# The key bias of the last attention's scores: from one-row products on TensorE to a fused add and maximum on VectorE

## What is computed

```python
qp = jnp.einsum('bsf,gf->bsg', q, Wq) + bq
kp = jnp.einsum('bsf,gf->bsg', k, Wk) + bk
vp = jnp.einsum('bsf,gf->bsg', v, Wv) + bv
attn = jax.nn.softmax(jnp.einsum('bqf,bkf->bqk', qp, kp), axis=-1)
return jnp.einsum('bqk,bkf->bqf', attn, vp) + q
```

## Time and profile before

| | |
|---|---|
| median of three runs | 1693.21 us (1687.25 to 1696.94) |
| the profiled execution | 1693.78 us |
| its span, first to last instruction | 1692.0 us |
| granted TensorE clock, mean | 0.977 |
| TensorE (PE) busy | 1595.8 us, 94% |
| VectorE (DVE) busy | 1112.9 us, 66% |
| ScalarE (ACT) busy | 991.6 us, 59% |
| GpSimd (POOL) busy | 271.6 us, 16% |

### The profile page before, as it was taken

One profiled execution on the slowest core, in us unless ns is written; L12 is line 12 of the kernel. 1 busy time (PEld: TensorE's weight loads), 2 busy tenths in 40 slices (PEclk: granted clock), 3 DMA queues, 4 the chain that ended last, 5 costly groups with the idle time before them and its releaser, 6 DMA issues.

```text
span 1692.0 us, 33823 instructions
## 1 busy us (share of the span) xinstructions
PE 1595.8 (94%) x12897; PEld 1029.4 (61%) x12897; DVE 1112.9 (66%) x2221; ACT 991.6 (59%) x2024; POOL 271.6 (16%) x344
## 2 busy tenths in 40 slices
PE   6789999999999999999999999999999989998987
PEld 5444445575767657575766657565656656564766
DVE  4566786867677676867677686867667675834433
ACT  3345667666667566656666666565756555664342
POOL 5200312021212011121203011100011010101110
PEclk9989999999999999999999999999999999997979
DMA  6913242536131331536131331336131320303200
GB/s 184 217 56 122 72 79 70 111 84 123 48 86 32 88 69 55 113 82 125 44 97 30 83 71 55 83 81 118 39 74 33 66 62 29 78 29 74 52 32 13
DMA packets 171647, 129.37 MB, mean 76 GB/s; under 512 B 40751, under 2 KB 161885, under 8 KB 171229
## 3 DMA queue, kind: packets, MB, share of 16 engines
q1 hardware_dynamic: 171421, 127.19, 32.0%
q10 hardware_dynamic: 64, 0.02, 0.0%
HBM read 78.92 MB, written 47.71 MB: 75 GB/s over the span
## 4 chain that ended last, share of the span: by engine, by line
PE 76%; DVE 11%; DMA 4%; ACT 4%; issue 2%; SPq 2%; DVEq 0%; ACTq 0%; POOLq 0%; POOL 0%
PE ps_o L1663 12%; PE ps_max L1634 11%; PE ps_s L1651 10%; PE ps_last L1582 10%; PE ps_last L1591 6%; DVE mxh L1320 6%; PE ps_pre L1446 4%; PE ps_cross L1550 4%; PE ps_pre L1454 3%; PE ps_cross L1536 3%; DMA den<-o_s 2%; PE ps_last L1454 2%; DVE mx L1248 2%; PE ps_last L1620 1%; PE ps_last L1604 1%
## 5 line engine op out<-in xcount | busy, mean ns | idle before, releaser
L1320 DVE TENSOR_REDUCE mxh<-ps_max 128x1 f32<-128x512 f32 x1024 | 655.6, 682 | 200.7 <-PE ps_max L1634 198.6
L1104 ACT ACTIVATE probs<-ps_s 128x512 f32<-128x512 f32 x1024 | 577.3, 596 | 235.4 <-PE ps_s L1651 177.5
L1634 PE MATMUL ps_max<-kst,qst 96*128 96x512 bf16 x1024 | 375.5, 388 | 23.3 <-DVE mxh L1320 16.9
L1651 PE MATMUL ps_s<-qst,kst 98*128 98x256 bf16 x2048 | 374.7, 276 | 11.0 <-ACT probs L1104 8.9
L1651 PEld LDWEIGHTS ps_s<-qst,kst 98*128 98x128 bf16 x2048 | 176.2, 98 | 162.4 <-ACT probs L1104 49.1
L1663 PE MATMUL ps_o<-probs,vg 128*17 128x256 f32 x4096 | 266.0, 382 | 0.0
L1634 PEld LDWEIGHTS ps_max<-kst,qst 96*128 96x128 bf16 x1024 | 97.1, 97 | 138.1 <-DVE mxh L1320 95.0
L1048 ACT ACTIVATE probs<-ps_cross 77x512 f32<-77x512 f32 x224 | 133.1, 594 | 72.5 <-PE ps_cross L1536 71.3
L1280 DVE SCALAR_TENSOR_TENSOR th<-th,gb 128x256 f32<-128x256 f32 x128 | 61.4, 480 | 160.4 <-ACT gb L1079 160.4
L1663 PEld LDWEIGHTS ps_o<-probs,vg 128*17 128x17 f32 x4096 | 97.7, 97 | 106.9 <-issue 43.6
L1582 PE MATMUL ps_last<-y_hi,wff_hi 128*128 128x256 f32 x448 | 139.9, 312 | 5.2 <-DVE y_lo L1274 4.3
(11 more groups left out here) (265 smaller groups left out, 2021.4 us busy)
## 6 DMA issues: line engine op xcount, KB each, us to landing
parts_s<-qk_parts SPq DMA_DIRECT2D x28, 384.0 KB, 3.9
o_s<-o_sb SPq DMA_DIRECT2D x64, 128.0 KB, 2.8
o_s<-o_sb SPq DMA_DIRECT2D x32, 256.0 KB, 2.2
oT<-o_s SPq DMA_DIRECT2D x62, 128.0 KB
den<-o_s SPq DMA_DIRECT2D x62, 128.0 KB
kst<-parts_s SPq DMA_DIRECT2D x16, 384.0 KB, 5.3
kst<-parts_s SPq DMA_DIRECT2D x48, 128.0 KB, 6.0
qst<-parts_s SPq DMA_DIRECT2D x64, 96.0 KB, 2.6
```

The source lines that it names most:

```text
L1104: nc.scalar.activation(probs[:, step % PR, 2 * pair:2 * pair + 2, :].rearrange("p j q -> p (j q)"), ps_s[pair][:, :], ACT.Exp, scale=SCALE ...
L1320: nc.vector.tensor_reduce(mxh[:, i // 2, i % 2:i % 2 + 1], ps_max[i % 2][:, :], AX_X, ALU.max).then_inc(g_mx, 1)
L1634: mm(ps_max[i % 2][:, :], qst[0:ROWS, h, q * P:(q + 1) * P], kst[0:ROWS, h, half * 512:(half + 1) * 512], start=True, stop=True).then_inc( ...
L1651: last = mm(ps_s[pair][:, j * CH:(j + 1) * CH], kst[:, h, kt * P:(kt + 1) * P], qst[:, h, :], start=True, stop=True)
```

## The change

The bias row is loaded to all 128 partitions, by a broadcast, instead of to one. The two one-row products of a chunk are gone, and so is the row of ones. On VectorE the reduction over both halves of the bank is replaced by two fused calls, one for each tile: each adds `m3_b` to the scores in PSUM, writes the sum back to the same place, and gives the maximum along the row into a column of `mx3`. As VectorE now reads `m3_b`, its next load waits for the last maximum of the preceding chunk (`c_mx3`) on SP.

```diff
-        ones = sb("ones", [1, P])
...
-        m3_b = sb("m3_b", [1, CTX])
+        m3_b = sb("m3_b", [P, CTX])
...
-                sp.dma_start(m3_b[:, :], m_s[D:D + 1, :].rearrange("a (b n) -> b a n", b=B)[b]).then_inc(c_tab, 16)
+                sp.wait_ge(c_mx3, o * TT)
+                sp.dma_start(m3_b[:, :], m_s[D:D + 1, :].rearrange("a (b n) -> b (a n)", b=B)[b].partition_broadcast(P)
+                             ).then_inc(c_tab, 16)
...
-            nc.gpsimd.memset(ones[:, :], 1.0).then_inc(s_const, 1)
...
-                nc.vector.tensor_reduce(mx3[:, :], bank_[:, :].rearrange("p (i n) -> p i n", i=TT)[:, :, 0:CTX],
-                                        AX_X, ALU.max).then_inc(c_mx3, 1)
-                dve.wait_ge(c_mx3, o + 1)
+                for i in range(TT):
+                    scores3 = bank_[:, i * CH:i * CH + CTX]
+                    nc.vector.tensor_tensor_reduce(scores3, scores3, m3_b[:, :], 1.0, -3.0e38, ALU.add, ALU.max,
+                                                   accum_out=mx3[:, i:i + 1]).then_inc(c_mx3, 1)
+                dve.wait_ge(c_mx3, (o + 1) * TT)
...
-                        mm(bank_[:, i * CH:i * CH + CTX], den2s[e][:, k, i * P:(i + 1) * P], m3[:, k, :],
-                           start=(k == 0), stop=False)
-                    last = mm(bank_[:, i * CH:i * CH + CTX], ones[:, :], m3_b[:, :], start=False, stop=True)
+                        last = mm(bank_[:, i * CH:i * CH + CTX], den2s[e][:, k, i * P:(i + 1) * P], m3[:, k, :],
+                                  start=(k == 0), stop=(k == KD - 1))
```

More of the change, by code:

```diff
@@ L790, in _ @@
             nc.gpsimd.memset(neghalf[:, :], -0.5).then_inc(s_const, 1)
-            nc.gpsimd.memset(ones[:, :], 1.0).then_inc(s_const, 1)
             v = v_sb[:, :, :, :]
             nc.gpsimd.memset(v, 0.0).then_inc(s_const, 1)
-            pool.wait_ge(s_const, 5)
+            pool.wait_ge(s_const, 4)
             nc.gpsimd.memset(v[:, :, :, DH:DH + 1], 1.0).then_inc(s_const, 1)
@@ L921, in _ @@
             act.wait_ge(s_cols, 1)
-            act.wait_ge(s_const, 6)
+            act.wait_ge(s_const, 5)
             def head():
```

## The result

Four executions of the changed kernel took 1666.29 to 1672.34 us, median 1667.69; four of the kernel before, on the same chip, had a median of 1693.46. The ratio is 0.9857 (95% interval 0.9821 to 0.9892), which is 24.2 us less. Two later comparisons gave 0.987 and 0.9864, 22.0 and 23.0 us less. The direction was right and the size too small.

The account below looks back on a forecast made before the run. TensorE was taken to bound the kernel (76% of the chain). Block gains of 15.4 us less 0.9 for the load gave 14.5, from 1693.78 to 1679.3 us; range 1671 to 1689.

Parts of the forecast that it names:

- TensorE's saving: Score blocks without one-row groups: 2.35 us falls to 1.17 in steady stages, 1.18 less; 1.19 less under LATE.
- The sum: Whole kernel: 8 x 1.16 + 4 x 0.95 + 3 x 0.78 = 15.4 us, less 0.9 for the bias load, gives 14.5.
- VectorE's pair: Two fused calls with maximum reads replace one 0.48 us reduction: 2 x (0.34 + 0.10) = 0.88 us, 0.40 more.
- The covers: VectorE's slack before TensorE needs the banks of the following maxima: 0.38 us in steady stages, 0.16 under LATE.
- `FINAL`'s 0.78: Chunk under FINAL: the values group waits for ScalarE's exponential, so 0.40 us is lost and 0.78 kept.
- The load: Bias row to 128 partitions on SP's queue delays the inverse sums' broadcast: 0.9 us charged once; bounds none and 3.6.
- The clock: Whole kernel: the forecast sum had no term for granted clock; more or fewer dips stood only among the rivals.
- Rival 1: VectorE's calls cost the upper price, so banks of the next maxima come late in 12 stages: 1687.9 us, chance 0.14.
- Rival 2: Next stage's projection waits for normalised rows set by SP's queue; six stages give nothing: 8.8 us gain, 1685.0, chance 0.12.
- Rival 3: Faster TensorE waits into half clock in eight more steady and LATE stages, 3.8 us each: 1709.7 us, chance 0.05.
- Rival 4: Two fewer dips of the clock than before: 1671.7 us, chance 0.08.
- the low price: VectorE's two calls at 2 x 0.34 us, reads hidden, 0.20 more than now; with a free load 1677.0 us.

Follow-up runs that it names:

- TensorE's part alone: Kernel before without the one-row products, nothing in their place, bias missing, old single reduction and one-partition load kept: 1671.09 us, ratio 0.9886 to before.
- VectorE's part alone: Changed kernel with each tile's one-row product put back, weights of zero; fused calls and broadcast load stay: 1691.46 us, ratio 1.0004 to the kernel before.
- the load later: Changed kernel with the bias row's broadcast moved behind the broadcast of the inverse sums on SP's queue: 1673.34 us, ratio 0.9891 to the kernel before.

## Why the prediction was right or wrong

**TensorE's saving: right.** Forecast 1.18 us a chunk, measured 1.20 and 1.21. The way it was found also held: the price of a group is read to the start of what follows it, and the time between records of one kind gives what remains when the other kind goes.

**The sum: the step that failed.** Sixteen blocks at 1.18 us are 18.9 us of TensorE time, and the sum let 14.5 of them reach the end: it took off 3.5 us as new waits for VectorE, ScalarE and the GELU chain at the blocks, and 0.9 for the load. New waits there are, some 2.2 us in all (below), but TensorE's idle time over the whole span did not grow: 96.2 us before, and in the three profiled executions of the change 96.1, 1663.6 - 1571.8 = 91.8 and 1668.9 - 1572.6 = 96.3. What TensorE waits more at the blocks it waits less elsewhere, so the whole of the 18.9 reached the end; where elsewhere is not settled, as such waits differ by some us from one execution to the next. The runs agree: TensorE's part alone, without VectorE's calls and the load, was no faster than the change. The second step that failed is that the clock was taken to stay as it was: it gave 2.8 us (0.8 to 4.8). Together with the mean of the idle time, 1.5 us less, these make 18.9 + 1.5 + 2.8 = 23.2, beside the 22.0 to 24.2 of the three comparisons.

**VectorE's pair: its price was mis-sized.** The step put 0.40 us on it. The calls take 0.18 more than the reduction did (0.69 against 0.51), just under the low bound of 0.20, and they start 0.09 later behind TensorE's next group, for which the step had no term: 0.27 together. The single call's 0.34 us was right:

```profile
L1295 DVE DVE_READ_ACCUMULATOR2_ANT mx<- x32: 137/140/142, 392.0 to 1662.4; 128x1 f32 x32
L1295 DVE CUSTOM_DVE_ANT_0 ps_last<-ps_last,m_b x30: 326/341/358, 391.8 to 1662.1; 128x154 f32<-128x154 f32 x30
```

These are ns of one, least, median and most. The read takes 0.14 us, but the next call starts with it, 0.25 us after the first call and so ahead of the first call's own end; only the last read stands alone. The Trainium skill, "VectorE: DVE Perf Modes", "Two Vector instructions with no wait between them", says that an operation that also writes out its accumulator is two instructions; the trace shows both. The prediction's estimate from that page, 0.95 us for the pair, adds their lengths; the trace has 0.69 from the first call to the next operation, since they overlap.

**The covers: right.** Those of 0.38 and 0.16 us stand. With 0.27 in place of 0.40, `LATE` pays 0.27 - 0.16 = 0.11, and 0.12 was measured; `ENDING` keeps 1.19 - 0.27 = 0.92, as measured. `FINAL`'s 0.78 came out to the digit, and chunk 14 gave 0.1, forecast nothing. The terms at the blocks become 8 x 1.20 + 4 x 1.09 + 0.78 + 0.92 + 0.1 + 0.96 = 16.7 us instead of 15.4, which leaves 18.9 - 16.7 = 2.2 for the new waits there.

**The load: a charge that no run shows.** It took the longer transfer of a broadcast beside the tables as the price. The kernel with VectorE's part alone, which has the load, is level with before (1.0004), and moving the load did not help. Both intervals are wider than 0.9 us, so a part of it may have been there.

**The clock: a term at nothing.** Taking the lost time off, the two kernels of the table with two one-row products have 1272.3 and 1270.5 us, the four with all of the change's work (the change, twice more, the load later) 1254.7, 1249.5, 1254.5 and 1253.4. The means differ by 18.4 us, the blocks' 18.9 within the scatter; over the timed executions the spans less the lost time differ by 19.5 (18.3 to 20.7). The clock comes beside it: 31.9 - 23.9 = 8.0 us in these single executions, but 2.8 in the timed ones, and these decide. The prediction's rivals 3 and 4 tied the half clock to TensorE's waits, by the projection at 603.80 alone, and so saw only that waits might come or go. That the products themselves can lower the clock was not among the cases; the kernel with six a chunk shows that they can. That the two a chunk did so is not shown.

The half clock behind the wait at 603.80 agrees with the Trainium skill, "TensorE: Matmul & The Clock Gate", Part 1, which has the clock released by how busy TensorE was. The six one-row products show the half clock with busy time of 7.00 in 7.00 us: being busy in the records did not by itself hold the clock at 2.4 GHz here, and the rows decide.

**The rivals.** Rival 1 (VectorE takes it back) falls with the price, and the waits for the maxima did not grow. Rival 2 (the next wait takes it back) falls: those waits did not grow. Rival 3 (the clock falls oftener) went the other way. Rival 4 (two dips fewer, 7.6 us, 1671.7 us in all) came nearest to the time, but by luck: the clock gave 2.8 us, not 7.6.

**The range.** Its low end put two dips fewer on the forecast alone. On the low price, 1677.0, the same two dips would have given 1669.4, about what was timed; two independent errors were not allowed to add. That sum would have come out by luck too, with a clock term that is too large and block terms that are too small.

**What stays open.** Whether the two one-row products a chunk cost the kernel before any clock, and where. None of its blocks of chunks 0 to 12 has a half clock in the 7 us behind it, and the 7 us behind chunk 13's block are low both before (0.80, from 1595.21) and after (0.85, from 1577.21). For it speak the 1.7 us between all executions with and without them; against it, that the kernels without them other than the change lost nearly as much as before, and that one of them lost 28.9 us in its trace. The change's 2.8 us can also come from its waits in the last stages, where TensorE runs at half clock in every trace.

## What to carry to other kernels

A product that uses one row of the array is not a small thing on a bound TensorE: here it cost its own time and the gaps on entering and leaving it, and with six a chunk clock for the work behind it. Where a bias can ride on an operation that another engine makes anyway, and that engine has cover, the whole price goes; read the cover from who waits next for that engine, and test it by making the engine slower. A new wait at one place need not lengthen the kernel: compare the bound engine's idle time over the whole span. When a change removes an unusual kind of product, compare the granted clock over the whole span, and not only behind waits, and over many executions: one trace of each kernel said 8 us here, the timed executions 3.

## What the runs showed of the hardware

One-row products lowered the granted clock from 2.4 to 1.2 GHz while TensorE was busy throughout by its records: with six a chunk the mean clock was 0.961 to 0.967 in four executions, with full-row products of zeros over about the same length 0.973 to 0.983 in six. Changing from 128-row to one-row products and back cost too: eight full records take 1.15 us, and with two one-row groups among them 2.35, where the starts of these groups stand 0.90 us in all ahead of what follows them. On VectorE a fused call with an accumulator costs 0.25 us to the next call's start for 154 columns, less than either its own 0.34 us or its two entries together.
